# A graph network on one core: the adjacency's zeros leave ScalarE, edge products go by type, and a scatter of records changes its block

## The chip, the cores and the metric

The kernel runs on one core of a Trainium2 chip. The metric is the device time of one execution in microseconds, here the median of several runs. A core has TensorE (PE, whose weight loads are listed as PEld), VectorE (DVE), ScalarE (ACT), GpSimd (POOL) and SyncE (SP, which issues DMAs). Each engine has a sequencer that goes through its instructions in order, register arithmetic and semaphore waits among them.

## What is computed

```python
def reference(x, src, dst, edge_weight, ...):          # 3125 nodes, 50000 edges sorted by dst, 128 features
    def step(h):                                        # L0: a gated step, 5 of them
        agg = segment_sum(h[dst] @ W_msg.T + b_msg, src)
        gi, gh = agg @ W_ih.T + b_ih, h @ W_hh.T + b_hh
        r, z = sigmoid(gi_r + gh_r), sigmoid(gi_z + gh_z)
        return (1 - z) * tanh(gi_n + r * gh_n) + z * h
    def layer(x, e_before):                             # L1: an edge layer, 3 of them
        e = relu(concat([x[src], x[dst], e_before]) @ We + be)   # the first has no e_before
        agg = segment_sum(e * edge_weight[:, None], dst)
        return relu(concat([x, agg]) @ Wn + bn), e
    x = layernorm(x + five_steps(x))
    x = layernorm(x + three_layers(x))
```

## The kernel before

The program is a chain of blocks; all engines meet between two of them. `step_tables` builds index tables (to 76 us of the profiled execution). `build_adjacency` builds a dense 3125 x 3125 matrix of edge counts. `gated_steps` runs the five steps on it. `add_and_norm` and `node_stage` are short. `edge_pass` runs three times, once a layer, and a last `add_and_norm` ends the kernel.

**The adjacency.** The matrix is built in 196 bands of 16 destinations. A band's sums lie in one of the eight PSUM banks, as 128 rows (16 destinations x 8 spans of sources) by 391 columns. One step takes at most 128 edges of one band: DVE makes two one-hot matrices, `dst_hot` (line 652, eight steps at once) and `src_hot` (line 660, one a step), and TensorE adds their product into the band's bank (line 681). There are 586 steps. Which band a step belongs to is known only at run time. TensorE reads the numbers from `band_i` into registers, 28 at a time (line 668), and forms the bank as `nth & 7`, so the address of each product is worked out by the sequencer. Line 679 waits for `dst_hot` every eight steps, line 680 and the wait behind it come every four. All these products have `start=False`, so a bank must hold zeros before its band begins: ScalarE writes zeros into it (line 691 for the first eight, line 704 afterwards) and counts them in `free`. When a band is complete ScalarE also copies its bank to `stage` (line 701), and SP sends the stage on into `adj` (line 711).

In the same block GpSimd issues 128 indirect DMAs (line 637). They scatter records of the first 128 tiles of edges to a place in device memory that groups them by the window of their source. Each waits until TensorE has done a further few steps. At the block's end SP waits for all of them and loads the sorted records into `sorted_in`, which occupies the memory of `record_of`. They are first read in `node_stage`, long after the gated steps.

**The edge layers.** A layer has 115 slots of four tiles (`QUAD`), 43 of them "sorted" and 72 "rest". In a slot, `products(q)` adds up four sums of 128 x 128 in one PSUM bank: for a sorted slot one float32 product with `p_sb` (line 1603), for every slot three bfloat16 products with the parts of `q_parts` (line 1610), and in layers 1 and 2 one float32 product of the edge features before with `w_c` (line 1614). A float32 product shows as two weight loads and two matmuls in the trace. The order is tile by tile, so the types alternate. `turn_and_sum` follows for the slot two earlier: four transposes (layers 0 and 1) and four float32 products `hot_w` by features (line 1634). The rows that a rest slot needs are gathered by GpSimd, four indirect DMAs a slot (line 1523). The sorted slots load the windows' numbers into TensorE's registers.

## Time and profile before

| | us |
|---|---|
| runs | 2203.95, 2204.12, 2209.13 (median 2204.12) |
| the profiled execution | 2204.84 |
| its span, first to last instruction | 2202.6 |
| adjacency, 76 to 306 | 230 |
| gated steps and what follows, 306 to 885 | 579 |
| the three edge passes, 917 to 1292, 1327 to 1744, 1780 to 2164 | 375, 417, 384 |

The profile is of one execution. Busy time is the time in which an engine worked; register operations, waits and branches of its sequencer are not counted as busy, and an idle time that no releaser explains is listed as "issue". Weight loads and matmuls are issued by the same sequencer. The granted clock of TensorE is given as a share of its full speed.

### The profile page before, as it was taken

To read this page: it belongs to the slowest core of one execution; us is meant where nothing else is said; L and a number is where in the kernel's file an instruction comes from. 1 tells how busy PE (TensorE), PEld (TensorE's weight loads), DVE (VectorE), ACT (ScalarE), POOL (GpSimd) and SP (SyncE) were. 2 spreads that over 40 slices of the span, in tenths; PEclk is the share of its full clock that TensorE was granted. 3 is DMA by queue.
4 is the path that set the end of the run, shared out by engine and by line. 5 is a ranking of instruction groups with operands and counts; after the bars stand their busy time and mean duration, and the time that the engine had idled before them with its cause. 6 is when DMAs were issued, how large, how long until landed. Compare 5 with 4: busy or idle time off the path is not lost. (4 is left out here: it accounts for less than half of the span.)

```text
span 2202.6 us, 47924 instructions
## 1 busy us (share of the span) xinstructions
PE 1899.2 (86%) x14264; PEld 1461.4 (66%) x14264; DVE 1403.0 (64%) x4662; ACT 647.0 (29%) x1271; POOL 1006.2 (46%) x1015
## 2 busy tenths in 40 slices
PE   6777669999999995588888877999999969999994
PEld 3433234545454543488888756999999859899993
DVE  6999741313132324588888854777777548788885
ACT  0168841212121211333333331333333322121111
POOL 0588700000000000377777725666666257777770
PEclk9688879999999997899999997999999989999998
DMA  3036770000000003445555525777777445555551
GB/s 99 14 78 108 108 64 0 0 0 0 0 0 0 0 0 126 163 149 151 155 155 149 148 90 151 216 217 215 217 216 217 127 116 157 142 158 146 157 150 36
DMA packets 193648, 242.12 MB, mean 110 GB/s; under 512 B 56276, under 2 KB 120047, under 8 KB 192799
## 3 DMA queue, kind: packets, MB, share of 16 engines
q1 hardware_dynamic: 161023, 172.73, 27.9%
q0 software_dynamic: 31840, 57.21, 11.1%
q10 hardware_dynamic: 576, 9.44, 1.1%
q8 instruction: 126, 2.06, 0.4%
q14 instruction: 83, 0.68, 0.1%
HBM read 149.75 MB, written 69.88 MB: 100 GB/s over the span
## 5 line engine op out<-in xcount | busy, mean ns | idle before, releaser
L1523 POOL DMA_INDIRECT rows<-p_dram,src_i x864 | 829.9, 961 | 348.0 <-issue 239.1
L1755 DVE TENSOR_TENSOR agg_t<-psum,agg_t 128x128 f32 x1380 | 393.3, 285 | 186.4 <-PE psum L1634 165.1
L1614 PE MATMUL psum<-w_c,before 128*128 128x128 f32 x1840 | 410.1, 305 | 0.0
L902 PE MATMUL psum<-adj,parts 128*128 (+2 forms) x1750 | 339.9, 352 | 5.3 <-ACT agg L981 4.4
L1603 PE MATMUL psum<-p_sb,pair_src 128*128 x1032 | 229.1, 306 | 108.2 <-DVE pair_dst L1729 65.4
L1688 ACT ACTIVATE rows<-rows 128x512 f32<-128x512 f32 x216 | 136.1, 630 | 578.8 <-DVE rows L1748 575.0
L1739 DVE TENSOR_SCALAR hot_w<-col_f,dst_loc,weight 128x128 f32<-128x128 f32 x864 | 302.7, 354 | 0.5
L1614 PEld LDWEIGHTS psum<-w_c,before 128*128 128x128 f32 x1840 | 282.4, 194 | 0.0
L902 PEld LDWEIGHTS psum<-adj,parts 128*128 128x128 f16 x1750 | 153.1, 98 | 190.9 <-issue 23.7
L1275 POOL MEMSET agg_t<- 128x3200 f32 x1 | 2.8, 2765 | 604.0 <-POOLq L1038 604.0
L1610 PE MATMUL psum<-q_parts,hot_all 128*128 x2592 | 252.3, 220 | 0.0
L850 DVE SCALAR_TENSOR_TENSOR gate_room<-psum,b_h,gate_room 128x512 f32<-128x512 f32 (+1 forms) x35 | 23.9, 683 | 349.0 <-ACT gate_room L988 349.0
L1603 PEld LDWEIGHTS psum<-p_sb,pair_src 128*128 128x128 f32 x1032 | 166.8, 203 | 119.1 <-issue 115.8
L1634 PE MATMUL psum<-hot_w,rows 128*128 128x128 f32 x1728 | 231.2, 277 | 0.0
L681 PE MATMUL psum<-src_hot,dst_hot 128*128 128x391 f16 x586 | 154.6, 399 | 70.6 <-DVE src_hot L660 33.3
L1634 PEld LDWEIGHTS psum<-hot_w,rows 128*128 128x128 f32 x1728 | 213.8, 195 | 0.0
L1610 PEld LDWEIGHTS psum<-q_parts,hot_all 128*128 128x128 bf16 x2592 | 201.9, 99 | 8.2
L1739 DVE TENSOR_SCALAR hot_w<-col_f,record_of 128x128 f32<-128x128 f32 x516 | 183.0, 361 | 11.6 <-PEq L151 11.2
L1610 PE MATMUL psum<-q_parts,pair_dst 128*128 x1548 | 181.6, 228 | 0.0
L637 POOL DMA_INDIRECT records<-record_of,place_i x128 | 158.4, 1237 | 45.3 <-PE psum L681 30.9
L681 PEld LDWEIGHTS psum<-src_hot,dst_hot 128*128 128x128 f16 x586 | 63.4, 108 | 161.9 <-issue 123.0
L1748 DVE TENSOR_TENSOR rows<-psum,rows 128x512 f32<-128x512 f32 x216 | 147.6, 684 | 36.4 <-DMA rows<-p_dram,src_i 36.2
(242 smaller groups left out, 2455.5 us busy)
## 6 DMA issues: line engine op xcount, KB each, us to landing
e_dram<-after SPq DMA_DIRECT2D x230, 256.0 KB
before<-e_dram SPq DMA_DIRECT2D x230, 256.0 KB
adj<-stage SPq DMA_DIRECT2D x196, 97.8 KB
pair_rows<-sorted_rows SPq DMA_DIRECT2D x129, 128.0 KB
rows<-p_dram,src_i POOLq DMA_INDIRECT x864
hot_all<-dst_rows ACTq DMA_DIRECT2D x2, 3072.0 KB, 15.0
p_dram<-p_sb SPq DMA_DIRECT2D x6, 384.0 KB
records<-record_of,place_i POOLq DMA_INDIRECT x128
```

Source lines behind the costliest of these rows:

```text
L637: nc.gpsimd.indirect_dma_start(out=keep["records"], out_offset=bass.IndirectOffsetOnAxis(ap=keep["place_i"][:, s:s + 1].bitcast(U32), axis=0),
L681: nc.tensor.matmul(psum[:, bass.ds(bank, 1), 0:SPAN], dst_hot[:, s // HOT_BATCH % BATCHES, s % HOT_BATCH // SIDE, :, s % SIDE], src_hot[:, ...
L902: mm = nc.tensor.matmul(psum[:, AGG_BANK, 0:n_cols], parts[:, w, part, :], adj[:, w, cols], start=(w == 0 and part == 0), stop=(w == WINDO ...
L1523: nc.gpsimd.indirect_dma_start(out=rows[:, b % ROWS, m * D:(m + 1) * D], out_offset=None, in_=p_dram, in_offset=bass.IndirectOffsetOnAxis( ...
L1603: nc.tensor.matmul(o, pair_src[:, i % PAIRS, m, :], t["p_sb"][:, bass.ds(values[m], 1), :], start=True, stop=False)
L1610: mm = nc.tensor.matmul(o, hot, t["q_parts"][:, bass.ds(window, 1), part, :], start=(part == 0 and i is None), stop=(part == 2 and e_befor ...
L1614: mm = nc.tensor.matmul(o, before[:, q % BEFORE, m * P:(m + 1) * P], w_c[:], start=False, stop=True)
L1634: mm = nc.tensor.matmul(psum[:, A_BANKS[q % len(A_BANKS)], m * P:(m + 1) * P], e[:, m * D:(m + 1) * D], hot_w[:, q % (LAG + 1), m, :], sta ...
L1688: nc.scalar.activation(e_of(q), source, ACT.Relu).then_inc(e_on, 1)
L1739: nc.vector.tensor_scalar(hot_w[:, q % (LAG + 1), m, :], keep["col_f"][:], of, weight, ALU.is_equal, ALU.mult).then_inc(hot_on, 1)
L1748: nc.vector.tensor_tensor(row, psum[:, E_BANKS[q % len(E_BANKS)], 0:WIDE], row, ALU.add).then_inc(added, 1)
L1755: nc.vector.tensor_tensor(a, psum[:, A_BANKS[q % len(A_BANKS)], m * P:(m + 1) * P], a, ALU.add).then_inc(agg_on, 1)
```

## The change

There are three parts. In the adjacency, ScalarE writes no zeros and the tile `zeros` and the semaphore `free` go. In their place a product with one column, `begin`, goes before every step's product, with the same weights: it writes column 511, which nobody reads, of the bank of the *following* band, and its `start=True` makes the next product that reaches a place in that bank overwrite rather than add. The first step begins the first band's bank as well, at a fixed address. TensorE waits on `staged`, the count of copied bands (ScalarE adds 7 to it at the start).

Second, the 128 scatters of records and the load of the sorted records stand in the block of `gated_steps`. GpSimd issues them there without waits between them, and SP waits for them there.

Third, in `products` a slot's four float32 products with `p_sb` go first, then the twelve bfloat16 products, then the four with `w_c`. One `start=True` a bank is left, on the first product.

```diff
--- before.py
+++ after.py
@@ -612,14 +612,12 @@
         dst_hot = sb("dst_hot", [P, BATCHES, HOT_BATCH // SIDE, P, SIDE], F16)
         lanes_h = sb("lanes_h", [P, P, SIDE], F16)
         stage = sb("stage", [P, STAGES, SPAN], F16)
-        zeros = sb("zeros", [P, SPAN], F16)
 
         zeroed = sem("zeroed")
         lanes_on = sem("lanes_on")
         src_on = sem("src_on")
         dst_on = sem("dst_on")
         counted = sem("counted_a")
-        free = sem("bank_free")
         staged = sem("staged")
         laid = [sem(f"laid{i}") for i in range(STAGES)]
 
@@ -627,17 +625,8 @@
 
         @block.gpsimd
         def _(pool):
-            nc.gpsimd.memset(zeros[:], 0.0).then_inc(zeroed, 1)
-            pool.wait_ge(zeroed, 1)
             last = (BANDS - 1) % SPANS * BAND + BAND
             nc.gpsimd.memset(adj[last:P, WINDOWS - 1, :], 0.0).then_inc(zeroed, 1)
-            for s in range(SORT_STEPS):
-                if s:
-                    pool.wait_ge(counted, s * (BAND_STEPS // SORT_STEPS))
-                nc.gpsimd.indirect_dma_start(
-                    out=keep["records"],
-                    out_offset=bass.IndirectOffsetOnAxis(ap=keep["place_i"][:, s:s + 1].bitcast(U32), axis=0),
-                    in_=keep["record_of"][:, s, :], in_offset=None).then_inc(keep["placed"], 16)
 
         @block.vector
         def _(dve):
@@ -662,6 +651,11 @@
 
         @block.tensor
         def _(pe):
+            def begin(bank, hot, s):
+
+                nc.tensor.matmul(psum[:, bank, CHUNK - 1:CHUNK], hot, src_hot[:, s % MOVES, 0:1],
+                                 start=True, stop=False, skip_group_check=True)
+
             for s in range(BAND_STEPS):
                 if s % PE_AT_ONCE == 0:
                     n = min(PE_AT_ONCE, BAND_STEPS - s)
@@ -672,23 +666,26 @@
                 nth = values[s % PE_AT_ONCE]
                 bank = nc.s_assert_within(nth & (BANKS - 1), 0, BANKS - 1,
                                           skip_runtime_bounds_check_because="three bits of the band's number")
+                following = nc.s_assert_within((nth + 1) & (BANKS - 1), 0, BANKS - 1,
+                                               skip_runtime_bounds_check_because="three bits of the next band's")
                 if s % HOT_BATCH == 0:
                     pe.wait_ge(dst_on, s // HOT_BATCH + 1)
                 if s % AT_A_TIME == 0:
                     last = min(s + AT_A_TIME, BAND_STEPS) - 1
                     pe.wait_ge(src_on, last + 1)
-                    pe.wait_ge(free, values[last % PE_AT_ONCE] & 255)
-                nc.tensor.matmul(psum[:, bass.ds(bank, 1), 0:SPAN],
-                                 dst_hot[:, s // HOT_BATCH % BATCHES, s % HOT_BATCH // SIDE, :, s % SIDE],
+                    pe.wait_ge(staged, values[last % PE_AT_ONCE] & 255)
+                hot = dst_hot[:, s // HOT_BATCH % BATCHES, s % HOT_BATCH // SIDE, :, s % SIDE]
+                if s == 0:
+                    begin(slice(1, 2), hot, s)
+                begin(bass.ds(following, 1), hot, s)
+                nc.tensor.matmul(psum[:, bass.ds(bank, 1), 0:SPAN], hot,
                                  src_hot[:, s % MOVES, 0:SPAN], start=False, stop=False,
                                  skip_group_check=True).then_inc(counted, 1)
 
         @block.scalar
         def _(act):
             nc.scalar.preload_act_table(ACT.Copy)
-            act.wait_ge(zeroed, 1)
-            for b in range(BANKS):
-                nc.scalar.copy(psum[:, (b + 1) % BANKS, 0:SPAN], zeros[:]).then_inc(free, 1)
+            act.sem_inc(staged, BANKS - 1)
             for g in range(BANDS):
                 if g % AT_ONCE == 0:
                     _, ends = nc.values_load_multi_w_load_instructions(
@@ -699,25 +696,17 @@
                 if g >= STAGES:
                     act.wait_ge(laid[g % STAGES], 16 * (g // STAGES))
                 nc.scalar.copy(stage[:, g % STAGES, :], psum[:, (g + 1) % BANKS, 0:SPAN]).then_inc(staged, 1)
-                if 1 <= g <= BANDS - BANKS:
-                    act.wait_ge(staged, g)
-                    nc.scalar.copy(psum[:, g % BANKS, 0:SPAN], zeros[:]).then_inc(free, 1)
 
         @block.sync
         def _(sp):
             for g in range(BANDS):
                 a = g % SPANS * BAND
-                sp.wait_ge(staged, g + 1)
+                sp.wait_ge(staged, BANKS + g)
                 sp.dma_start(adj[a:a + BAND, g // SPANS, :].rearrange("d (a b) -> d a b", a=SPANS),
                              stage[:, g % STAGES, :]).then_inc(laid[g % STAGES], 16)
             for i in range(STAGES):
                 sp.wait_ge(laid[i], 16 * len(range(i, BANDS, STAGES)))
-            sp.wait_ge(zeroed, 2)
-            sp.wait_ge(keep["placed"], 16 * SORT_STEPS)
-            with nc.allow_non_contiguous_dma(reason="a lane's record of every tile"):
-                sp.dma_start(keep["sorted_in"][:],
-                             keep["records"][0:SORT_TILES * P, 0:3].rearrange("(j p) f -> p j f", p=P)
-                             ).then_inc(keep["sorted_got"], 16)
+            sp.wait_ge(zeroed, 1)
 
 
 def chunk_width(c):
@@ -783,6 +772,22 @@
         at = {}
 
         block = ctx.enter_context(nc.Block())
+
+        @block.gpsimd
+        def _(pool):
+            for s in range(SORT_STEPS):
+                nc.gpsimd.indirect_dma_start(
+                    out=keep["records"],
+                    out_offset=bass.IndirectOffsetOnAxis(ap=keep["place_i"][:, s:s + 1].bitcast(U32), axis=0),
+                    in_=keep["record_of"][:, s, :], in_offset=None).then_inc(keep["placed"], 16)
+
+        @block.sync
+        def _(sp):
+            sp.wait_ge(keep["placed"], 16 * SORT_STEPS)
+            with nc.allow_non_contiguous_dma(reason="a lane's record of every tile"):
+                sp.dma_start(keep["sorted_in"][:],
+                             keep["records"][0:SORT_TILES * P, 0:3].rearrange("(j p) f -> p j f", p=P)
+                             ).then_inc(keep["sorted_got"], 16)
 
         @block.vector
         def _(dve):
@@ -1597,22 +1602,28 @@
                     pe.wait_ge(hot_t_on, b + 1)
                 if e_before is not None:
                     pe.wait_ge(before_in[q % BEFORE], 16 * (q // BEFORE + 1))
+                def sums(m):
+                    return psum[:, E_BANKS[q % len(E_BANKS)], m * D:(m + 1) * D]
+
+                if i is not None:
+                    for m in range(QUAD):
+                        nc.tensor.matmul(sums(m), pair_src[:, i % PAIRS, m, :],
+                                         t["p_sb"][:, bass.ds(values[m], 1), :],
+                                         start=(m == 0), stop=False, skip_group_check=True)
                 for m in range(QUAD):
-                    o = psum[:, E_BANKS[q % len(E_BANKS)], m * D:(m + 1) * D]
                     if i is not None:
-                        nc.tensor.matmul(o, pair_src[:, i % PAIRS, m, :], t["p_sb"][:, bass.ds(values[m], 1), :],
-                                         start=True, stop=False)
                         hot, window = pair_dst[:, i % PAIRS, m, :], values[QUAD + m]
                     else:
                         s = (b * QUAD + m) * P
                         hot, window = hot_all[:, s:s + P], values[(b % 2 + 2) * QUAD + m]
                     for part in range(3):
-                        mm = nc.tensor.matmul(o, hot, t["q_parts"][:, bass.ds(window, 1), part, :],
-                                              start=(part == 0 and i is None),
-                                              stop=(part == 2 and e_before is None))
-                    if e_before is not None:
-                        mm = nc.tensor.matmul(o, before[:, q % BEFORE, m * P:(m + 1) * P], w_c[:],
-                                              start=False, stop=True)
+                        mm = nc.tensor.matmul(sums(m), hot, t["q_parts"][:, bass.ds(window, 1), part, :],
+                                              start=(i is None and m == 0 and part == 0),
+                                              stop=(part == 2 and e_before is None), skip_group_check=True)
+                if e_before is not None:
+                    for m in range(QUAD):
+                        mm = nc.tensor.matmul(sums(m), before[:, q % BEFORE, m * P:(m + 1) * P], w_c[:],
+                                              start=False, stop=True, skip_group_check=True)
                 mm.then_inc(spread, 1)
 
             def turn_and_sum(q):
```

## Rows read from the trace of the kernel before

**Rows 1.** Table of windows: span; PE, PEld, DVE, ACT, POOL busy; clock, DMA share.

```profile
76.00:306.00 230.00, 154.99 (x587) 63.45 (x587) 194.46 (x661) 164.39 (x393) 160.16 (x129) 0.83 0.50 88
306.00:885.00 579.00, 539.54 (x2472) 270.37 (x2472) 176.70 (x346) 111.87 (x188) 0.00 (x0) 0.97 0.07 15
...
917.00:1292.00 375.00, 318.55 (x3111) 299.93 (x3110) 312.88 (x1140) 124.79 (x233) 274.81 (x285) 0.95 0.49 147
...
1327.00:1744.00 417.00, 403.46 (x4033) 396.53 (x4033) 296.41 (x1066) 127.99 (x233) 271.38 (x285) 0.98 0.70 204
...
1780.00:2164.00 384.00, 357.35 (x3573) 349.04 (x3573) 297.91 (x1066) 71.07 (x117) 273.95 (x285) 0.97 0.51 142
```

**Rows 2.** Waits of the adjacency, 79:296: engine, line, releaser: total us, times, longest.

```profile
PE psum L681 <- DVE src_hot L660: 33.3, 26, 2.4
...
PE psum L681 <- ACT psum L704: 24.5, 17, 2.7
```

**Rows 3.** Groups by line in 79:296: busy us, mean ns, idle before.

```profile
L637 POOL DMA_INDIRECT records<-record_of,place_i x128 | 158.4, 1237 | 45.3 <-PE psum L681 30.9 <-issue 14.4
...
L660 DVE TENSOR_SCALAR src_hot<-gate_room 128x392 f16<-128x392 f16 x581 | 152.5, 321 | 23.2 <-PE psum L681 22.5
...
L652 DVE TENSOR_TENSOR dst_hot<-lanes_h,gate_room 128x1024 f16<-128x1024 f16 x73 | 49.7, 681 | 0.0
```

**Rows 4.** Line 681, PE's sequencer (PEldq): ns least, median, most; first and last.

```profile
L681 PEldq ALU_OP  x586: 32/32/32, 78.8 to 295.3; - x196
L681 PEldq FUSED_REGOPS  x586: 46/46/46, 78.9 to 295.4; - x196
```

**Rows 5.** Lines 668, 679 and 680, PE's sequencer, each its own line's view.

```profile
L668 PEldq TENSOR_LOAD <-band_i x21: 1875/2212/2662, 74.6 to 285.1; - x21
...
L679 PEldq EVENT_SEMAPHORE  x74: 51/51/51, 78.6 to 294.9; - x74
...
L680 PEldq ALU_OP  x147: 32/32/42, 78.7 to 295.0; - x147
```

**Rows 6.** Timeline of weight loads, 181:186: start, length, engine, line, count, idle before.

```profile
182.33 0.75 PEld L681 LDWEIGHTS psum<-src_hot,dst_hot 128*128 128x128 f16 x4 [0.32 <-issue]
185.41 0.54 PEld L681 LDWEIGHTS psum<-src_hot,dst_hot 128*128 128x128 f16 x3 [2.34 <-issue]
```

**Rows 7.** Timeline of weight loads, 923:925.2, an edge pass just after a wait.

```profile
923.73 1.52 PEld L1610 LDWEIGHTS psum<-q_parts,hot_all 128*128 128x128 bf16 x12
```

**Rows 8.** Timeline, the adjacency's two ends.

```profile
75.77 3.88 DVE L660 TENSOR_SCALAR src_hot<-gate_room 128x392 f16<-128x392 f16 x8
...
79.02 4.60 PE L681 MATMUL psum<-src_hot,dst_hot 128*128 128x391 f16 x16 [8.39 <-ACT psum L691]
...
294.03 1.77 PE L681 MATMUL psum<-src_hot,dst_hot 128*128 128x391 f16 x6 [0.59 <-ACT psum L704]
...
298.45 0.87 ACT L701 CAST stage<-psum 128x391 f16<-128x391 f32 x2 [0.59 <-DMA adj<-stage]
...
305.53 0.37 PE L925 MATMUL psum<-ident,largest 128*3 128x128 f32 x1 [9.73 <-PEq L601]
```

**Rows 9.** Timeline of products, 1400.2:1404.5, in edge layer 1.

```profile
1400.48 1.06 PE L1634 MATMUL psum<-hot_w,rows 128*128 128x128 f32 x8
1401.37 0.33 PE L1610 MATMUL psum<-q_parts,hot_all 128*128 x3
1401.54 0.44 PE L1614 MATMUL psum<-w_c,before 128*128 128x128 f32 x2
1401.82 0.33 PE L1610 MATMUL psum<-q_parts,hot_all 128*128 x3
```

**Rows 10.** Groups by line: 917:1292, then 1327:1744, then (POOL) 1780:2164.

```profile
L1610 PE MATMUL psum<-q_parts,hot_all 128*128 x864 | 61.6, 221 | 0.0
...
L1610 PE MATMUL psum<-q_parts,hot_all 128*128 x864 | 95.3, 219 | 0.0
...
L1523 POOL DMA_INDIRECT rows<-p_dram,src_i x284 | 273.0, 961 | 98.6 <-issue 79.3 <-PE psum L1634 15.2 <-PE psum L1614 4.1
```

## Prediction

> **What bounds the kernel now.** I read the table of windows first, because each part of the change belongs to another stage [rows 1]. The gated steps are TensorE's: 539.5 of 579 us busy, GpSimd idle throughout, DMA at 0.07. Edge layer 1 is TensorE's as well (403 of 417), layer 2 nearly so (357 of 384), and in layer 0 DVE (313 of 375) is nearer to the bound than TensorE's array. The adjacency looks different: in 230 us no engine is busy for more than DVE's 194, and TensorE has 155.
>
> So there I read the waits [rows 2]. They blame DVE for 33.3 us in 26 waits and ScalarE's zeros for 24.5 us in 17, none longer than 2.7. These waits have another owner for the most part. TensorE's sequencer loads 28 band numbers 21 times, each load taking about 2.2 us [rows 5]; a gap of 2.34 us stands between two groups of weight loads where such a load falls [rows 6], and in it TensorE starts nothing. That is 21 x 2.2 = 46 us.
>
> Then the lines of one product. For each of the 586 steps the sequencer runs one ALU_OP and one FUSED_REGOPS (the masking, then the multiply-add of the address) before the weight load [rows 4]. The reader is to see the pitch: four weight loads in a row span 0.75 us with the last one's 0.10 in it, so (0.75 - 0.10) / 3 = 0.217 us a step [rows 6], though nothing is waited for inside that group. In an edge pass, just after a wait, twelve bfloat16 products with one register operation each are pitched (1.52 - 0.10) / 11 = 0.129 us [rows 7], where the same products run three in (0.33 - 0.22) / 2 = 0.056 us when the sequencer is ahead (0.22 is the mean of one) [rows 9, 10]. So a register operation holds the sequencer for about 0.217 - 0.129 = 0.088 us, and a load and matmul for about 0.129 - 0.088 = 0.041 us (estimates from these rows).
>
> With these the sequencer's own time in the adjacency is 586 x 0.217 = 127, the loads 46, and 147 + 74 waits [rows 5] at 0.088, 19.5: together 193 us. The products last from 79.0 to about 295.8 [rows 8], 217 us. TensorE's sequencer is the bound, with 24 us of true waits and slow-clock stretches beside it.
>
> **The zeros and the begins.** Removed: 196 ScalarE writes. ScalarE was not the bound, so their price is in the 24 us of waits, and at the two ends. At the start the first product waited 8.39 us for the zeros; now it needs the first four `src_hot`, of a group that began at 75.8, so it can start at about 77 instead of 79. At the end ScalarE was behind: its last copy ended at 299.3, 3.5 us after the last product, and the next block began at 305.5 [rows 8]. With a slower TensorE it is not behind: the last copy ends about 0.8 us after the product and the same 6.2 us follow, less a little, so 6.5 us in place of 9.7.
>
> Added: in each step a second weight load and matmul, 0.041 us, with a bank of its own, `(nth + 1) & 7`. The trace does not show that address. The nearest row is the address of `nth & 7`: a masking that stands by itself, and a fused multiply-add [rows 4]. The addition comes before the masking and so can't be in the fused operation; I take three register operations, 3 x 0.088 = 0.264. The lower bound is the two of the row, 0.176, the upper four, 0.352; nothing of it at all is a rival below. The step becomes 0.217 + 0.264 + 0.041 = 0.522, and 586 x 0.305 = 179 us come onto the sequencer: 193 + 179 = 372. Nothing covers this, because the sequencer is the bound already; the 24 us of waits go under it. DVE (194 us of work in all [rows 1], nearly all of it lines 660 and 652 [rows 3]) and ScalarE (now one copy a band) now wait for TensorE, and the wait on `staged` is met long before. The next block begins at 77 + 372 + 6.5 = 455.5 in place of 305.5: **+150 us**. By two operations it would be 586 x 0.088 = 52 us less, by four 52 us more.
>
> The Trainium skill ("TensorE: Matmul & The Clock Gate", Back-to-back issue gap) says that matmuls never start less than about 25 ns apart however few columns they have; 586 one-column products would by that page's floor be 586 x 0.025 = 15 us (an estimate). The rows above differ: a step of 391 columns is pitched by its register operations.
>
> **The scatters.** Removed from the adjacency: 128 issues on GpSimd, 158 us busy and 45 us of waits [rows 3], off the path. Moved: behind the block's start, ahead of nothing else on GpSimd, which has no work until 885 [rows 1]. Without the waits for TensorE they take 158 + 14 = 173 us at most, so they end far ahead of the block, and SP's load of the records follows there on DMA queues at 0.07. SP has no other work in the gated steps. The price is zero, covered by GpSimd's idle 579 us; if that cover were gone it would be those 173 us. Taking them out of the adjacency gives nothing either, since TensorE's sequencer never waits for them. How far the scatters hold up DVE in the gated steps is not in the trace; DVE is busy for 177 of 579 us there beside a TensorE that is busy for 540, so I take 0, with bounds of -5 and +5 us.
>
> **Edge products by type.** Products start at 1401.37 (three bfloat16), 1401.54 (two halves of a float32) and 1401.82 (the next bfloat16) [rows 9]. Three bfloat16 take 0.17, 0.056 each; two float32 halves take 0.28, but eight in a row start 0.111 apart ((1401.37 - 1400.48) / 8), which would be 0.222. So each change from bfloat16 to float32 costs 0.055 us. A slot of layers 1 and 2 has four such changes and keeps one: 3 x 0.055 = 0.165 us. That is 115 x 0.165 = 19 us a layer, and 43 x 0.165 = 7 us in layer 0's sorted slots. Layer 1 should give nearly all of it. In layer 2 GpSimd's gathers are the next bound: 273.0 busy and 79.3 of issue [rows 10] are 352 of 384 us, so about 365 can be reached and I take 14. In layer 0 DVE and GpSimd cover it, and I take 0. With a little lost, **-30 us**, bounds 0 and -45.
>
> **Sum.** 2204.8 (the profiled execution, 0.7 above the median) + 150 - 30 = 2324.8, so a median of **2324 us**.
>
> **Rivals.**
> - *Two register operations a begin*, as for `nth & 7`. For it: that row is the only one there is. Against: one addition more. Time 2324 - 52 = 2272. *Four or more*, with a move: 2376.
> - *The begins are nearly free, and the kernel gets faster.* If the second address costs no register operation (made once, or kept from the step before), the stream is 193 + 586 x 0.041 = 217 us, the block begins at 77 + 217 + 6.5 = 300.5, 5 us earlier, and with the edges the time is 2204 - 5 - 30 = 2169. It decides below an added 0.1 us a step, where 586 x 0.1 = 59 us are met by the edges' 30, the 24 us of waits and 5 us at the two ends. Against: every step's band is another register, and the 586 + 586 operations show that nothing is kept now. The Trainium skill's floor of 25 ns ("TensorE: Matmul & The Clock Gate", as above) speaks for this case; no row here shows it.
> - *Twelve bfloat16 products in a row outrun the sequencer.* At 0.129 against 0.056 a slot could lose 12 x 0.073 = 0.88 us, 230 slots 200 us. Against: layer 0's rest slots have their twelve in a row already, and 864 of them are busy 61.6 us, 0.86 a slot [rows 10], as 11 x 0.056 + 0.22 = 0.84 asks. If a fifth of it came, the edges would give nothing: 2354.
>
> **How the numbers follow.** Three operations 0.68, two 0.16, four or more 0.05, the edges outrun 0.02, the free begin 0.08, no measurable change 0.01 (it needs the added 0.1 by chance). I predict the likeliest, 2324; its own range is 2305 to 2360, by the edges' bounds and the small terms. To hold 8 in 10 the range takes in the case of two operations with the edges' gain in full: 2272 less 15 is 2257. Four operations and the free begin stay out, so 2257 to 2362. A measurement of this kernel tells about 0.3%, 7 us. Slower 0.91, same 0.01, faster 0.08.
>
> **What would show it.** In the adjacency about 1173 matmuls with a pitch near 0.52 us a step, more than 586 register operations of either kind on line 681 or the helper's, GpSimd idle there, DVE waiting for TensorE, and the next block at about 455. GpSimd's 128 scatters right after it, ended 173 us later or sooner, and the gated steps as long as before. In layer 1 the bfloat16 products of rest slots at about 61 us in place of 95.3 [rows 10], and the pass at about 398 us. The prediction is wrong if the step's pitch stays near 0.26 us.

## The result and the profile after

The changed kernel takes 2370.07 us in the median of four runs (2368.21 to 2372.59), the kernel before 2204.73 us (2203.95 to 2209.13): a ratio of 1.0746, with a 95% interval of 1.0728 to 1.0765. The direction was forecast; 2370 us lies 46 us above the predicted 2324 us and 8 us above the range's upper end. The profiled execution took 2369.6 us, its span 2367.6 us.

The table of windows by stage comes first, with the columns of [rows 1]: adjacency, gated steps, the three edge passes.

```profile
76.50:479.00 402.50, 328.33 (x1174) 121.96 (x1174) 225.14 (x657) 95.33 (x197) 0.00 (x0) 0.50 0.19 50
479.00:1059.50 580.50, 538.75 (x2473) 269.53 (x2473) 176.96 (x347) 112.47 (x188) 126.72 (x128) 0.97 0.08 15
1092.00:1466.60 374.60, 317.10 (x3111) 298.25 (x3111) 313.30 (x1142) 124.80 (x233) 274.11 (x285) 0.94 0.50 148
1505.00:1905.50 400.50, 387.35 (x4033) 382.97 (x4033) 297.81 (x1066) 127.93 (x233) 274.65 (x285) 0.98 0.72 212
1943.50:2327.50 384.00, 347.51 (x3572) 342.94 (x3572) 295.82 (x1066) 70.67 (x117) 272.54 (x285) 0.95 0.52 142
```

Against [rows 1] the adjacency is the stage that grew: its next block starts at 479.0 instead of 305.5 us, which is +173.4. The gated steps take 0.8 us more, the three passes -0.5, -16.5 and +1.3, and the short stages between and behind them 6.6 together. That makes 165, the difference of the spans. TensorE's granted clock in the adjacency is 0.50, the lower of its two levels, where it was 0.83. The array is busy for 328 us at that slow clock, and still idle for 74 of 402.

The ends of the stage, in the timeline:

```profile
72.18 2.81 DVE L633 COPY lanes_h<-gate_room 128x256 f16<-128x256 f16 x1 [0.32 <-PEq L165]
...
76.89 0.18 PE L656 MATMUL psum<-src_hot,dst_hot 128*128 128x1 f16 x1 [8.68 <-DVE src_hot L649]
...
474.11 1.06 ACT L698 CAST stage<-psum 128x391 f16<-128x391 f32 x2 [0.85 <-PE psum L681]
...
474.15 0.51 PE L681 MATMUL psum<-src_hot,dst_hot 128*128 128x391 f16 x1
...
478.99 0.37 PE L930 MATMUL psum<-ident,largest 128*3 128x128 f32 x1 [4.34 <-PEq L601]
```

The products begin 2 us earlier, at the time predicted, but by chance: the whole block began 2.4 us earlier in this execution. DVE's first copy started at 72.18, and before the change at 74.60:

```profile
74.60 0.53 DVE L644 COPY lanes_h<-gate_room 128x256 f16<-128x256 f16 x1 [0.33 <-PEq L165]
```

From there to the first product pass 4.7 us now and passed 4.4 before [rows 8], so the start gained nothing without the zeros. ScalarE's last copy ends half a microsecond behind the last product. The products take 398 us; I had 372. What the sequencer does in a step stands in the view of the `begin`'s line (656), with least, median and most ns of a record:

```profile
L656 PEldq ALU_OP  x1172: 36/36/36, 76.9 to 473.7; - x196
L656 PEld LDWEIGHTS psum<-src_hot,dst_hot x587: 102/104/105, 76.9 to 473.9; 128*128 128x128 f16 x196
L656 PE MATMUL psum<-src_hot,dst_hot x587: 181/183/184, 76.9 to 473.9; 128*128 128x1 f16 x196
L656 PEldq FUSED_REGOPS  x586: 60/60/60, 77.1 to 473.8; - x196
```

Line 681 keeps its own two operations, as in [rows 4]. So a `begin` has three register operations of its own: addition, masking, address. The likeliest case came true. The pitch shows in the timeline of weight loads:

```profile
201.39 0.10 PEld L656 LDWEIGHTS psum<-src_hot,dst_hot 128*128 128x128 f16 x1 [0.26 <-issue]
201.61 0.10 PEld L681 LDWEIGHTS psum<-src_hot,dst_hot 128*128 128x128 f16 x1
201.94 0.10 PEld L656 LDWEIGHTS psum<-src_hot,dst_hot 128*128 128x128 f16 x1 [0.23 <-issue]
202.15 0.10 PEld L681 LDWEIGHTS psum<-src_hot,dst_hot 128*128 128x128 f16 x1
202.52 0.10 PEld L656 LDWEIGHTS psum<-src_hot,dst_hot 128*128 128x128 f16 x1 [0.26 <-issue]
```

From one `begin` to the next 0.55 us pass; the median over the stage is 0.548, where a step took 0.217 [rows 6] and I had forecast 0.522. In a step without a wait the records start 0.097 us behind each ALU_OP of the `begin`, 0.109 behind its FUSED_REGOPS, and 0.029 behind its weight load: 0.332 added. The Trainium skill ("Perfetto Trace Analysis", Sequencer-only Instruction) says that the profile shows only the execution of a sequencer's operation and leaves out what precedes and follows it. These rows agree: records of 36 and 60 ns hold the sequencer for 97 and 109.

No other engine holds the stream up. The waits of the stage, by engine, line and releaser (total us, times, longest):

```profile
ACT stage L698 <- PE psum L681: 304.7, 193, 23.5
...
DVE src_hot L649 <- PE psum L681: 162.4, 454, 2.9
```

In the edge passes, groups by line (layer 1's three kinds of product, then GpSimd's gathers in layer 2, then its scatters in the gated block):

```profile
L1625 PE MATMUL psum<-w_c,before 128*128 128x128 f32 x920 | 128.9, 283 | 0.0
...
L1620 PE MATMUL psum<-q_parts,hot_all 128*128 x864 | 61.0, 220 | 0.0
...
L1610 PE MATMUL psum<-p_sb,pair_src 128*128 x344 | 47.6, 283 | 22.3 <-DMA before<-e_dram 13.3 <-DVE pair_dst L1740 8.8 <-issue 0.3
```

```profile
L1528 POOL DMA_INDIRECT rows<-p_dram,src_i x284 | 272.3, 959 | 99.5 <-issue 78.1 <-PE psum L1645 20.5 <-PE psum L1625 0.9
```

```profile
L779 POOL DMA_INDIRECT records<-record_of,place_i x128 | 126.7, 990 | 446.3 <-issue 446.3
```

The bfloat16 products of layer 1's rest slots are busy 61.0 us instead of 95.3 [rows 10], as forecast (61). In layer 2 TensorE's busy time is 347.5 us instead of 357.4, and the pass is no shorter. GpSimd's 288 gathers there, with the start of the first and the last, before and after:

```profile
L1523 POOL DMA_INDIRECT rows<-p_dram,src_i x288: 942/947/1246, 1774.3 to 2151.7; - x144
...
L1528 POOL DMA_INDIRECT rows<-p_dram,src_i x288: 943/947/1174, 1936.5 to 2314.6; - x144
```

The scatters ran from 479.8 to 646.7, 990 ns each (1237 in the adjacency [rows 3]), and nobody waited for them.

### The profile page after: what moved, and what is told of

Its sections match the earlier page's. It is cut to its first block and busy times, and to the rows that moved or that the text cites. A ratio compares the mean times of both kernels' runs of the same rounds, so it can differ in the third digit from the quotient of the medians.

```text
span 2367.6 us, 50659 instructions
## 1 busy us (share of the span) xinstructions
PE 2046.3 (86%) x14851; PEld 1498.7 (63%) x14851; DVE 1436.8 (61%) x4662; ACT 577.8 (24%) x1075; POOL 975.3 (41%) x1014
## 5 line engine op out<-in xcount | busy, mean ns | idle before, releaser
L681 PE MATMUL psum<-src_hot,dst_hot 128*128 128x391 f16 x586 | 296.1, 505 | 23.6 <-issue 1.4
L779 POOL DMA_INDIRECT records<-record_of,place_i x128 | 126.7, 990 | 446.3 <-issue 446.3
L649 DVE TENSOR_SCALAR src_hot<-gate_room 128x392 f16<-128x392 f16 x586 | 187.4, 322 | 166.0 <-PE psum L681 162.4
L1625 PE MATMUL psum<-w_c,before 128*128 128x128 f32 x1840 | 261.8, 286 | 0.0
L1610 PE MATMUL psum<-p_sb,pair_src 128*128 x1032 | 153.8, 296 | 118.9 <-DVE pair_dst L1740 61.6
L1625 PEld LDWEIGHTS psum<-w_c,before 128*128 128x128 f32 x1840 | 230.5, 197 | 0.0
L1610 PEld LDWEIGHTS psum<-p_sb,pair_src 128*128 128x128 f32 x1032 | 136.4, 206 | 127.4 <-issue 126.7
L1620 PE MATMUL psum<-q_parts,hot_all 128*128 x2592 | 183.2, 220 | 0.0
L698 ACT CAST stage<-psum 128x391 f16<-128x391 f32 x196 | 95.3, 486 | 306.5 <-PE psum L681 304.7
```

What stands on the lines that cost most here:

```text
L649: nc.vector.tensor_scalar(src_hot[:, s % MOVES, :], span_h, place_f[:, s:s + 1], None, ALU.is_equal).then_inc(src_on, 1)
L681: nc.tensor.matmul(psum[:, bass.ds(bank, 1), 0:SPAN], hot, src_hot[:, s % MOVES, 0:SPAN], start=False, stop=False, skip_group_check=True). ...
L1610: nc.tensor.matmul(sums(m), pair_src[:, i % PAIRS, m, :], t["p_sb"][:, bass.ds(values[m], 1), :], start=(m == 0), stop=False, skip_group_c ...
L1620: mm = nc.tensor.matmul(sums(m), hot, t["q_parts"][:, bass.ds(window, 1), part, :], start=(i is None and m == 0 and part == 0), stop=(part ...
L1625: mm = nc.tensor.matmul(sums(m), before[:, q % BEFORE, m * P:(m + 1) * P], w_c[:], start=False, stop=True, skip_group_check=True)
```

## The experiments

**The parts alone.** Three kernels each take one part of the diff: the begins in place of the zeros, the products by type, the scatters in the gated block.

> The begins in place of ScalarE's zeros, alone; the scatters stay in the adjacency and the edge products in the old order. Theory A (TensorE's sequencer sets the adjacency; a begin brings it three register operations, a weight load and a matmul): the whole loss of the changed kernel's adjacency is here, the next block begins at 479 us and the time is 2204.7 + 173 = 2378 us. Rival B (part of that loss comes from the other two parts): clearly under 2370 us.

> The edge products by type, alone. Theory A (GpSimd's gathers already set layers 0 and 2, so only layer 1 gains): layer 1 is 16 us shorter, layers 0 and 2 within 2 us, the time 2188 us. Rival B (the prediction: layer 2 gains as well, and the changed kernel's slow adjacency hid it): 2175 us. Rival C (twelve bfloat16 products in a row outrun the sequencer): 2200 us or more.

> The 128 scatters in the block of the gated steps, alone. Theory A (neither place is on the path): 2204.7 within 3 us, the adjacency as long as before. Rival B (the scatters hold up DVE in the gated steps): 5 us or more slower. Rival C (without them the adjacency's engines run more freely): 3 us or more faster, by an earlier start of the gated steps.

| part alone | us, median | ratio to before, interval | gated steps start | edge passes |
|---|---|---|---|---|
| begins | 2383.87 | 1.0791, 1.0765 to 1.0818 | 481.7 | 373.0, 415.3, 383.9 |
| by type | 2187.08 | 0.9909, 0.9895 to 0.9924 | 303.0 | 372.8, 400.3, 383.2 |
| scatters | 2205.41 | 0.9990, 0.9980 to 1.0001 | 306.2 | 374.6, 415.7, 386.1 |

The whole loss is the begins', the scatters are worth nothing that can be measured, and the products by type gain 19 us, nearly all of it in layer 1. That part alone is faster than either kernel.

**What a register operation costs.** The one-column product stays, but goes into the step's own bank and starts nothing, so that the addition and the second masking fall away. Eight products at fixed banks begin all banks once, at the first step; no bank is cleared between bands.

```diff
                 if s == 0:
-                    begin(slice(1, 2), hot, s)
-                begin(bass.ds(following, 1), hot, s)
+                    for b in range(BANKS):
+                        begin(slice(b, b + 1), hot, s)
+                begin(bass.ds(bank, 1), hot, s, False)        # start=False
```

> The changed kernel with every step's one-column product, but into the bank of the step's own product and without the start flag (the resetting is left out as in the kernel without begins). The masked number is formed once for both, so a step has three register operations (after: five), two loads and two matmuls. Theory A (register operations on the sequencer): 0.217 + 0.095 + 0.03 = 0.342 us a step, the gated steps begin near 77 + 586 x 0.342 + 68 + 5 = 350 us, the time is about 2241 us. Rival B (the second weight load and the slow array set the step): the step stays near 0.55 us and the time near 2370 us.

It took 2247.54 us in one run (before on the same chip 2205.93); the gated steps start at 362.0. The views of the two lines:

```profile
L656 PEldq ALU_OP  x586: 32/32/32, 76.9 to 355.1; - x196
L656 PEldq FUSED_REGOPS  x586: 55/55/65, 77.0 to 355.2; - x196
```

```profile
L682 PEldq FUSED_REGOPS  x586: 42/42/42, 77.1 to 355.3; - x196
```

One masking serves both products, two address operations remain. A step without a wait takes 0.346 us (0.093 for the ALU_OP, 0.105 and 0.092 for the two others, 0.028 behind each weight load): 0.129 over the step of before, for one more register operation and one more load and product. The product as such is cheap, and the register operations of its address are not; the changed kernel's two further ones make up the 0.202 between 0.346 and 0.548. The slow clock is not the cause: 363 of these steps ran at the full granted clock and 222 at the lower level, and a step without a wait takes the same 0.346 us at either. The Trainium skill ("TensorE: Matmul & The Clock Gate", Back-to-back issue gap) has a floor of about 25 ns between matmuls. The trace agrees where no address has to be worked out: the eight products at fixed banks start 0.026 to 0.028 us apart, behind a first gap of 0.046. That floor was never what held the stream.

**What the zeros had cost.** The changed kernel without its begins, apart from eight fixed ones at the first step: no bank is cleared between bands.

```diff
                 if s == 0:
-                    begin(slice(1, 2), hot, s)
-                begin(bass.ds(following, 1), hot, s)
+                    for b in range(BANKS):
+                        begin(slice(b, b + 1), hot, s)
```

> The changed kernel without the begins: the eight banks are begun once at the start, and later bands add onto earlier ones, so the resetting of the banks is left out. Theory A (sequencer): a step has two register operations, one load and one matmul, 0.217 us; the stream is 193 us or DVE's 194, the gated steps begin near 283 us in place of 479, and the time is about 2174 us. Rival B (the loss lies elsewhere in the adjacency): they begin later than 300.

It took 2191.9 us in one run, with the gated steps from 303.3. That is the time of the products by type alone, 2187 and 303.0, where ScalarE writes every zero. So the expectation fell: to be rid of the zeros gains nothing. The waits of this kernel, in the adjacency:

```profile
PE psum L681 <- DVE src_hot L649: 29.6, 20, 2.6
PE psum L681 <- ACT stage L698: 27.1, 15, 2.7
```

They are as large as in [rows 2], though ScalarE has half the work. Most of these 57 us are register loads of over 2 us each. The rest can be told by the sequencer's records, each of which starts when its wait is over. In the kernel before, 24 waits for a bank (15 us beyond the operation itself) end 0.04 us behind a zero write of ScalarE, all of them later than 200 us. Here 15 such waits (11 us) end 0.04 us behind a copy to `stage`, and the copies in turn wait for the transfers into `adj`. The window 200 to 293 of the products by type alone, then the same window and a wait of this kernel:

```profile
200.00:293.00 93.00, 64.91 (x231) 25.55 (x229) 75.36 (x255) 86.24 (x210) 60.22 (x54) 0.80 0.70 115
...
200.00:293.00 93.00, 63.00 (x232) 25.89 (x231) 73.68 (x255) 48.48 (x103) 0.00 (x0) 0.82 0.92 112
...
ACT stage L698 <- DMA adj<-stage: 30.8, 63, 1.6
```

With the zeros ScalarE is busy for 86 of those 93 us. Without them it is busy for 48, but the DMA engines are busy for 0.92 of the stretch where they were for 0.70, and about as many products (232 and 231) fall into it. So the zeros did hold TensorE up there, and behind them stood the transfers at almost the same pace.

**Layer 2.** Two kernels take work from two engines there. In the first the changed kernel leaves out the products with `w_c` in layers 1 and 2, 920 float32 halves and about 130 us of TensorE's work a layer:

```diff
-                if e_before is not None:
-                    for m in range(QUAD):
-                        mm = nc.tensor.matmul(sums(m), before[...], w_c[:], ...)
```

> The changed kernel without the products of the edge features before with w_c in layers 1 and 2 (that term is left out of the sums; its loads and waits stay). They take TensorE 115 x 0.89 = 102 us a layer. Theory A (GpSimd's 288 gathers, 1.25 us each with their gaps, are 361 us, with about 12 us of waits at the start): layer 1 falls from 400 to no less than 375, layer 2 stays above 373, the time is about 2370 - 25 - 8 = 2337 us. Rival B (TensorE's array or sequencer sets these layers): both fall by 60 us or more, under 2250 us.

2350.49 us in one run, 20 less than the changed kernel: layer 1 took 387.0, layer 2 375.6, layer 0 as before 374.8. In layer 2, 133 us of TensorE's work are worth 8 us. GpSimd has the same row as before, without the wait for TensorE:

```profile
L1528 POOL DMA_INDIRECT rows<-p_dram,src_i x288 | 276.3, 959 | 102.0 <-issue 81.7 <-PE psum L1641 10.7 <-POOLq L151 6.8
```

The second takes the products by type alone and, in layer 2 only, puts plain transfers of fixed rows in the place of half of GpSimd's gathers, so that those rows are not the ones asked for:

```diff
+                    if nth == 2 and m >= 2:
+                        nc.gpsimd.dma_start(rows[...], p_dram[0:P, :]).then_inc(rows_in[b % ROWS], 16)
+                        continue
```

> The products by type alone, and in layer 2 half of the gathers of a tile's rest rows are replaced by plain transfers of fixed rows that GpSimd starts (that part of the computation is changed). Theory A, GpSimd's gathers set layer 2's length: layer 2 falls from 383 us to between 355 and 372 us, and the whole from 2187 to between 2158 and 2177 us; layers 0 and 1 stay at 373 and 400 us. Rival, the coupling of TensorE and VectorE sets it: layer 2 stays within 3 us of 383 us and the whole within 4 us of 2187 us.

2158.03 us (2157.39 to 2159.18), ratio 0.9777 (0.9760 to 0.9794); layer 2 takes 347.6 us instead of 383.2, the other two 374.6 and 401.5. GpSimd's groups by line, then the window of the pass:

```profile
L1527 POOL DMA_INDIRECT rows<-p_dram,src_i x142 | 140.9, 992 | 101.0 <-PE psum L1644 65.4 <-issue 33.5 <-PE psum L1624 2.1
L1524 POOL DMA_DIRECT2D rows<-p_dram x142 | 87.9, 639 | 4.0 <-PE psum L1624 4.0
```

```profile
1769.00:2117.00 348.00, 337.50 (x3572) 332.98 (x3572) 295.45 (x1066) 71.59 (x117) 228.01 (x284) 0.98 0.55 156
```

Now GpSimd waits for TensorE (65 us), and TensorE is busy for 337.5 of 348: the bound has changed sides. The pass fell even below the 355 expected. The gathers set layer 2, and the gain of the products by type lies idle there until gathers are cheaper.

**Fewer register operations a step.** If those alone are the bound of the adjacency before the change, a bank's number made in advance must pay. DVE masks the numbers in the block before, and TensorE loads 28 banks and, in a second register load, the seven numbers for the waits.

```diff
-                nth = values[s % PE_AT_ONCE]
-                bank = nc.s_assert_within(nth & (BANKS - 1), 0, BANKS - 1, ...)
+                    _, bands = nc.values_load_multi_w_load_instructions(keep["band_w"][0:1, ...], ...)
+                bank = values[s % PE_AT_ONCE]
```

> The zeros of before, the edge products by type, and in the adjacency TensorE reads bank numbers that DVE has masked beforehand, so that a step takes one register operation in place of two; band numbers for the waits come from a second, short table. Theory A (the sequencer sets the adjacency): its own time falls from 193 to about 586 x 0.124 + 46 + 13 + 20 = 152 us, DVE's 194 us become the bound, the gated steps begin about 20 us earlier (near 285), and with layer 1's 16 us the time is about 2168 us. Rival B (ScalarE's copies and zeros or DVE set it): the adjacency is as long as before, 2188 us.

2203.73 us (2200.72 to 2213.2), ratio 0.9992 (0.9977 to 1.0006), which is 17 us slower than the products by type alone. A product's operations were down to one, 0.124 us apart where the sequencer ran ahead, and a run of steps to 0.166 us each. That is the array's own pace at the full granted clock; at the lower level it is 0.327. But the second load, of seven values, took nearly as long as the first:

```profile
L680 PEldq TENSOR_LOAD <-band_w x21: 1082/1847/2362, 76.7 to 298.8; - x21
```

So the next theory was that a register load has a fixed price. Two kernels take the products by type with 12 and with 32 numbers in a load, by one constant.

```diff
-        ... AT_ONCE, PE_AT_ONCE, AT_A_TIME = ..., 28, 28, 4
+        ... AT_ONCE, PE_AT_ONCE, AT_A_TIME = ..., 28, 12, 4
```

> The products by type alone, with 12 numbers in one register load where 28 stood: 49 loads in the adjacency where 21 stood. Theory A, the price of a register load hardly depends on how many values it takes: 28 more loads at 1.8 to 2.2 us put the gated stages' start 50 to 62 us later than 303.0 us, and the whole at 2237 to 2249 us. Rival, the price goes by the value: the start moves by less than 10 us, and the whole stays under 2197 us.

> The products by type alone, with 32 numbers in one register load where 28 stood: 19 loads in the adjacency where 21 stood. Theory A, the price of a register load hardly depends on how many values it takes (about 2 us each): the gated stages start some 2 to 5 us earlier than 303.0 us and the whole is 2182 to 2185 us. Rival, the price goes by the value: no change, 303 us and 2187 us within 1.5 us.

They took 2193.14 us (two runs) and 2189.85 us (2188.0 to 2195.06), the gated steps from 303.6 and 301.4. The price goes by the value, and the fixed price is refuted. With 12 numbers, then with 32:

```profile
L668 PEldq TENSOR_LOAD <-band_i x49: 843/1025/1398, 74.7 to 289.8; - x49
```

```profile
L668 PEldq TENSOR_LOAD <-band_i x19: 1357/2451/2918, 72.2 to 287.8; - x19
```

Seven values should then cost some 0.65 us, not 1.85. The next kernel puts the banks of 24 steps and their six numbers for the waits side by side, in one load of 30.

```diff
+            groups = keep["band_w"][:].rearrange("p (n k) -> p n k", k=30)
...
+                    n = 24 + -(-min(PE_AT_ONCE, BAND_STEPS - s) // AT_A_TIME)
+                    at = s // PE_AT_ONCE * 30
+                    _, values = nc.values_load_multi_w_load_instructions(keep["band_w"][0:1, at:at + n], ...)
+                    bands = values[PE_AT_ONCE:]
```

> The products by type alone, and the bank's number is made once for all steps by VectorE in the block before, so that a product's address costs one register operation where it cost two. The banks of 24 steps and the six numbers for the waits stand side by side and come in one register load of 30 numbers (25 loads where 21 stood, each some 0.15 us longer). Theory A, TensorE's sequencer bounds the adjacency: the step falls from 0.217 to 0.166 us, which is 586 x 0.051 = 30 us less, the loads take 25 x 2.4 = 60 us where they took 47, so the products take 198 us where they took 215, and the whole 2170 us; 2165 to 2178 us is its range. Rival, VectorE's twelve src_hot slots and its 194 us of work set the pace as soon as the sequencer is a little faster: the products stay at 210 to 217 us and the whole at 2182 to 2190 us.

2241.64 us (2236.61 to 2242.2), ratio 1.0166 (1.0149 to 1.0182): worse than both expected. Every second load stopped the sequencer for 8 us, the others for 2.5 to 3.1. The loads' line, and the timeline of weight loads around one load of either kind:

```profile
L686 PEldq TENSOR_LOAD <-band_w x25: 2502/3104/8527, 72.2 to 337.5; - x25
```

```profile
151.55 0.46 PEld L699 LDWEIGHTS psum<-src_hot,dst_hot 128*128 128x128 f16 x3 [7.95 <-issue]
...
155.45 1.76 PEld L699 LDWEIGHTS psum<-src_hot,dst_hot 128*128 128x128 f16 x11 [0.18 <-issue]
159.53 1.11 PEld L699 LDWEIGHTS psum<-src_hot,dst_hot 128*128 128x128 f16 x8 [2.32 <-issue]
```

Thirty numbers are 120 bytes, so every second group begins off a multiple of 16. The last kernel pads a group to 32 numbers, and loads 30 as before.

```diff
-            groups = keep["band_w"][:].rearrange("p (n k) -> p n k", k=30)
+            groups = keep["band_w"][:].rearrange("p (n k) -> p n k", k=32)
-                    at = s // PE_AT_ONCE * 30
+                    at = s // PE_AT_ONCE * 32
```

> The packed table with two unused numbers behind each group of 30, so that a group begins every 128 bytes and not every 120. Before, the register loads alternated between about 2.6 and 8 us; loads that began every 112, 128 or 48 bytes never did, and those of 7 values, which began every 28 bytes, were cheap every fourth time (every 112 bytes). Theory A, a register load is dear where its first number does not lie on a multiple of 16 bytes: now none is, all 25 take 2.3 to 3.1 us, the 12 dear ones give back 12 x 5.2 = 62 us, the products take 200 to 207 us, and the whole is 2171 to 2182 us. Rival 1, the alternation has another cause (30 values, or every second load whatever its place): loads of 7 us or more remain and the whole stays over 2220 us. Rival 2, the loads are cheap but VectorE's pace takes over: the products stay at 210 to 217 us and the whole at 2182 to 2190 us.

```profile
L686 PEldq TENSOR_LOAD <-band_w x25: 2379/2749/3017, 74.5 to 285.3; - x25
```

2181.87 us (2180.55 to 2190.55), ratio 0.9901 (0.9885 to 0.9917). No dear load is left, so the place was the cause, and rival 1 is refuted. The median lies where the ranges of theory A and rival 2 meet, but the rows decide for rival 2 and for more than it said. The products take 213 us. The sequencer's register loads grew, 25 of 2.75 us (69 us) where 21 of 2.2 were 47. Two other engines have nearly as much to do in those 213 us, DVE 199 (149.7 and 49.6) and ScalarE 195 (98.3 and 96.8):

```profile
L677 DVE TENSOR_SCALAR src_hot<-gate_room 128x392 f16<-128x392 f16 x584 | 149.7, 320 | 20.5 <-PE psum L699 20.0
...
L719 ACT CAST stage<-psum 128x391 f16<-128x391 f32 x195 | 98.3, 504 | 54.5 <-PE psum L699 45.6 <-DMA adj<-stage 4.8 <-issue 2.7
L722 ACT CAST psum<-zeros 128x391 f32<-128x391 f16 x188 | 96.8, 515 | 0.0
...
L669 DVE TENSOR_TENSOR dst_hot<-lanes_h,gate_room 128x1024 f16<-128x1024 f16 x73 | 49.6, 680 | 0.0
```

The two halves of the stage, and the waits of its products:

```profile
78.00:192.00 114.00, 75.89 (x350) 38.06 (x351) 111.04 (x395) 70.40 (x170) 92.94 (x66) 0.88 0.40 74
192.00:292.00 100.00, 60.02 (x238) 26.82 (x236) 76.91 (x263) 89.30 (x217) 71.30 (x63) 0.82 0.79 113
...
PE psum L699 <- DVE src_hot L677: 39.8, 21, 3.0
PE psum L699 <- ACT psum L722: 34.3, 29, 2.8
```

DVE is busy for 111 of the first 114 us and ScalarE for 89 of the last 100. In the sequencer's records 41 waits end 0.04 us behind a write of DVE, 34 of them before 192 us, and 29 behind a zero write of ScalarE, all of them after it. So the sequencer is no longer the bound here: DVE is in the first half, and ScalarE with its zeros and copies in the second. With the products by type alone (0.9909) this kernel is level: two versions beat both kernels by about 1%, and the runs don't separate them.

## Why the forecast was right in its direction and 46 us short

- **The mechanism held.** "I take three register operations" is what line 656 shows; the begins alone lose 178 us and carry the whole loss. Nothing covered them: DVE waits for TensorE for 162 us in 454 waits after the change, ScalarE for 305 us.
- **The step that failed first is the size "0.217 + 0.264 + 0.041 = 0.522, and 586 x 0.305 = 179 us".** A step takes 0.548, and 0.331 are added: 586 x 0.026 = 15 us more. The register operation was estimated too low, at 0.088; here it holds the sequencer for 0.097 to 0.109, and for 0.092 to 0.105 in the kernel with the same bank. The load and product were put too high, at 0.041; here they are 0.029. Operations of differing length had been given one mean price.
- **"193 + 179 = 372" was short by 11 us more.** 586 x 0.548 = 321, the 20 loads between the products, 2.15 each with what follows the record, are 43, and with the waits' 22 that makes 386; the products take 398, the last half microsecond of it the last product alone. The 11 us that are left are some 200 short interruptions in the sequencer's records, 0.05 us each, whose cause stays open. The block's end was 2 us shorter than I had it. Together the stage grew by 173 and not by 150.
- **"About 365 can be reached and I take 14" failed for layer 2.** It set GpSimd's floor from the 284 gathers that the window's row lists, 273 + 79. The layer has 288 at a pitch of 1.25 us, some 361 us from the first to the last without any stop. Before the change they took 377.4 from first start to last, after it 378.1. Layer 0 is alike (374.3 and 373.1). So layer 2 stood at GpSimd's pace already, stops at the start included, as the two kernels on layer 2 show. Layer 1 gave 16.5 of the 19 us.
- **The rest is 7 us** in the gated steps and the short stages, none over about 3 and not studied.
- **The "24 us of true waits"** did go under the longer stream, as forecast: 0.3 us of waits are left in the sequencer's records. Before, 15 of the 24 were waits for ScalarE's zeros, as the prediction allowed, but all in the last 95 us, where "TensorE's sequencer is the bound" was not the whole truth. What it did not see is that the transfers into `adj` stood behind the zeros, so that their removal could not have paid even with free begins.
- **"It can start at about 77 instead of 79"** came true by luck: the block began earlier in that execution, and from its beginning the first product came no sooner.
- **Rivals.** Two operations (2272) and nearly free begins (2169) were wrong; the 0.1 us from which the latter decides was passed by the address alone. Twelve bfloat16 products in a row did not outrun the sequencer: 61.0 us for 864.
- **The scatters** cost and gave nothing, as said.

## What to carry to other kernels

Where a stream of small products has addresses known only at run time, count the sequencer's register operations first: each held this one for 0.09 to 0.11 us, three times what a further product and its weight load cost. A product added "for free" is priced by its address, and one with the address of its neighbour cost 0.129 us a step where one with an address of its own cost 0.331. An engine's floor is the count of all its operations times their pitch, start-up waits included; a sum of busy and idle time over the window's listed rows can fall short of it. And work taken off one engine pays only up to the next thing that waits: behind the zeros stood the transfers, at almost the same pace.

## What the runs showed of the hardware

- A register load of TensorE took 1.03 us for 12 numbers, 2.2 for 28 and 2.45 for 32, some 0.075 us a number between 12 and 32. One whose first number did not lie on a multiple of 16 bytes took about 8 us for 30 numbers, against 2.7 on such a multiple: with groups of 120 bytes every second load was dear, with groups of 48, 112 and 128 bytes none. The seven-value loads, which step by 28 bytes, took 1.08 to 1.42 us every fourth time, where they lie on a multiple of 16, and 1.7 to 2.4 otherwise; even the cheap ones took more than the 0.65 us that the price by the number gives.
- A masking that two addresses share is done once: the kernel with the same bank has 586 ALU_OPs for 1172 addressed products.
- A product of 391 columns with its weight load was pitched at 0.166 us at the full granted clock and at 0.327 at the lower level, where nothing else held it (the kernel with the bank table).
- A scatter of 128 records took GpSimd 990 ns in the gated steps and 1237 in the adjacency; a plain transfer that it starts took 639 where a gather took 959 to 992.
